# Weights of three experts loaded a stage earlier, into dead buffers, and a second buffer in the expert loop

## The reference

```python
# delta rule layer, its tail
enc = o.reshape(b, t, VAL_DIM) @ Wo
x = x + enc
h2 = _layernorm(x, ln2_g, ln2_b)
x_out = jax.nn.gelu(h2 @ W2 + b2, approximate=False) + x
...
# mixture of experts: 8 experts, each token goes to one
for ei in range(e):
    h = jax.nn.gelu(xf @ W1[ei] + b1[ei], approximate=False)   # 256 -> 1024
    y = h @ W2[ei] + b2[ei]                                    # 1024 -> 256
    mask = (idxf == ei).astype(xf.dtype)
    out = out + y * (gf * mask)[:, None]
```

## Time and profile before

| | |
|---|---|
| median of 3 runs | 699.14 us (697.95 to 700.17) |
| profiled execution | 700.65 us, of it the span 698.9 us |
| TensorE busy, share of the span | 610.0 us, 87% |
| DVE / ScalarE / Gpsimd busy | 55% / 48% / 18% |
| mean granted clock of TensorE | 0.935 |
| stage e ends, stage f starts | 578.36, 579.72 us |
| DMA moved, mean | 40.78 MB, 58 GB/s |

### The profile page before, as it was taken

One profiled execution on the slowest core, in us unless ns is written; L12 is line 12 of the kernel. 1 busy time (PEld: TensorE's weight loads), 2 busy tenths in 40 slices (PEclk: granted clock), 3 DMA queues, 4 the chain that ended last, 5 costly groups with the idle time before them and its releaser, 6 DMA issues. The chain is left out here.

```text
span 698.9 us, 20484 instructions
## 1 busy us (share of the span) xinstructions
PE 610.0 (87%) x8420; PEld 455.6 (65%) x8420; DVE 382.4 (55%) x911; ACT 333.5 (48%) x927; POOL 128.1 (18%) x192
## 2 busy tenths in 40 slices
PE   4779998999899999999777988988798986599995
PEld 2447666665466666666656765465798876498995
DVE  6426788875434545552267884879565783011211
ACT  1325655553444455444246764655365263144451
POOL 2002221001200000000223443424520204011111
PEclk9869999999999999999868999999789996799999
DMA  5950000000700000000230000000000007996110
GB/s 152 306 203 2 3 2 2 2 17 27 165 2 1 2 1 2 1 1 2 61 104 1 3 3 1 0 3 3 2 3 1 1 1 278 323 378 197 26 33 19
DMA packets 32717, 40.78 MB, mean 58 GB/s; under 512 B 8031, under 2 KB 28000, under 8 KB 32385
## 3 DMA queue, kind: packets, MB, share of 16 engines
q1 hardware_dynamic: 28672, 32.24, 14.2%
q0 software_dynamic: 1520, 4.38, 1.9%
q10 hardware_dynamic: 2448, 3.09, 1.6%
HBM read 35.33 MB, written 4.90 MB: 58 GB/s over the span
## 5 line engine op out<-in xcount | busy, mean ns | idle before, releaser
L390 ACT ACTIVATE a_pr<-a_bank,a_nms 128x160 f32<-128x160 f32 x128 | 49.2, 392 | 41.2 <-DVE a_nms L726 38.1
L2485 ACT ACTIVATE f_hb<-f_bank,cols 128x128 f32<-128x128 f32 x96 | 31.1, 368 | 59.7 <-PE f_bank L2596 38.1
L2596 PE MATMUL f_bank<-f_xts,f_w 128*128 x384 | 46.9, 282 | 9.0 <-ACT f_hb L2485 8.2
L2596 PEld LDWEIGHTS f_bank<-f_xts,f_w 128*128 128x128 f32 x384 | 46.4, 198 | 10.0 <-ACT f_hb L2485 8.4
L2606 PE MATMUL f_bank<-f_w,f_hb 128*128 128x256 f32 x192 | 46.4, 385 | 0.8 <-DVE f_yb L2565 0.8
L630 DVE TENSOR_REDUCE a_negmx<-a_bank 128x2 f32<-128x320 f32 x64 | 30.4, 475 | 22.8 <-PE a_bank L863 22.8
L2606 PEld LDWEIGHTS f_bank<-f_w,f_hb 128*128 128x128 f32 x192 | 35.3, 194 | 5.1 <-DVE f_yb L2565 1.2
L2557 DVE TENSOR_SCALAR f_xts<-f_bank 128x256 f32 x12 | 5.1, 424 | 60.8 <-PE f_bank L2588 60.8
L360 POOL TENSOR_TENSOR a_spr<-a_linv,a_hm 128x128 f32<-128x128 f32 x32 | 12.1, 400 | 123.9 <-DVE a_linv L679 111.1
L974 PE MATMUL a_bank<-b_wq,a_xtb 128*128 128x512 f32 x64 | 30.6, 624 | 2.9 <-ACT a_ct L483 2.9
L627 DVE COPY a_pt<-a_bank 128x512 f32<-128x512 f32 (+1 forms) x48 | 28.5, 593 | 7.9 <-PE a_bank L872 5.3
(11 more groups left out here) (406 smaller groups left out, 1457.8 us busy)
## 6 DMA issues: line engine op xcount, KB each, us to landing
f_w<-in_f_w SPq DMA_DIRECT2D x16, 1024.0 KB, 10.8
a_ct<-in_ctxt SPq DMA_DIRECT2D x15, 160.0 KB, 4.4
slots<-a_zero POOLq DMA_DIRECT2D x1, 2210.0 KB, 12.1
f_xs<-slots ACTq DMA_DIRECT2D x14, 130.0 KB, 2.4
rows<-in_rows SPq DMA_DIRECT2D x1, 1096.0 KB, 8.1
x<-in_x SPq DMA_DIRECT2D x2, 512.0 KB, 5.4
b_wq<-in_b_wq SPq DMA_DIRECT2D x1, 1024.0 KB, 6.2
b_wk<-in_b_wk SPq DMA_DIRECT2D x1, 1024.0 KB, 8.3
```

Of the source, the lines that this page charges most:

```text
L390: i = act.activation(pr[:, p, j, k, :], s_bank[j][:, k * KW:(k + 1) * KW], ACT.Exp, bias=nms[:, p, j, k:k + 1], accum_out=rsum[:, p, 2 * j ...
L2485: act.activation(hb[:, m, :], bank[m % 4][:, 0:P], ACT.Gelu, bias=c.col("f_b1", e * FC + m)).then_inc(z["act"], 1)
L2596: j = pe.matmul(bank[m % 4][:, 0:P], w1[:, e, kk, m * P:(m + 1) * P], xts[:, bass.ds(i % 2, 1), kk, :].rearrange("p b n -> p (b n)"), star ...
```

## The change

Three experts' weights are loaded in stage e, by a new program of SP, into buffers whose contents are no longer needed: expert 0 into `d_k` (where `aT` was) and the buffer of `lT`, once `abd` and the last factor products are done; expert 1 into `d_v`, after the last gated product; expert 2 into `e_gate`, after the last encoding. SP waits for all six transfers before the stage's end. For this `lT` becomes `c.e_lt` and stage f runs inside `held_d`. Expert 3's room is `e_wqkv` and `e_ht`, filled in stage f; experts 4 to 7 have buffers of their own.

In stage f SP waits for the scatters, loads tile 1's rows and then tile 0's, waits for tile 1's, and loads experts 3 to 7. b2 is loaded by Gpsimd into `e_xl`, and its landing counts on `stored`. `next_rows` on ScalarE moves from behind the fourth GELU to behind the eighth. DVE adds b2 into a new buffer `hy` without waiting for the store (its semaphore `yb2` is now what TensorE waits for), and waits for `rows_out` only before the product that writes `f_yb`. Gpsimd waits for the store of the tile before at the start of its tile instead of at the end of the one before.

```diff
         z = sems("eps proj ... lgs nmr ids ew")
...
+        @block.sync
+        def _(sp):
+            def weights(e):
+                sp.dma_start(c.f_w1[e], c.d["f_w1"][e, :, :].rearrange("(k p) n -> p k n", p=P)).then_inc(z["ew"], 16)
+                sp.dma_start(c.f_w2[e], c.d["f_w2"][e, :, :].rearrange("(k p) n -> p k n", p=P)).then_inc(z["ew"], 16)
+            sp.wait_ge(z["abd"], 4)
+            sp.wait_ge(z["y"], 4 * (LEVELS - 1))
+            weights(0)
+            sp.wait_ge(z["og"], NT)
+            weights(1)
+            sp.wait_ge(z["enc"], NT)
+            weights(2)
+            sp.wait_ge(z["ew"], 16 * 6)
...
         @block.sync
         def _(sp):
-            for e in range(E):
-                if e > 1:
+            sp.wait_ge(z["scattered"], 16 * NT)
+            sp.dma_start(xs[:, 1, :], slots[P:2 * P, :]).then_inc(z["xs"], 16)
+            sp.dma_start(xs[:, 0, :], slots[0:P, :]).then_inc(z["xs0"], 16)
+            sp.wait_ge(z["xs"], 16)
+            for e in range(3, E):
+                if e > 4:
                     sp.wait_ge(s_w[e - 2], 32)
-                if e == 3:
-                    sp.wait_ge(z["xs0"], 16)
-                    sp.wait_ge(z["xs"], 16)
...
         @block.gpsimd
         def _(pool):
             pool.sem_inc(z["row"], 1)
+            pool.dma_start(b2[:, :], c.d["f_b2"].partition_broadcast(P)).then_inc(z["stored"], 16)
...
             def write(e, i):
                 pool.wait_ge(z["nrm"], i + 1)
                 pool.nop(nofuse=True)
+                pool.wait_ge(z["stored"], i * 16 + 16)
+                pool.nop(nofuse=True)
+                pool.sem_inc(z["rows_out"], 1)
                 pool.tensor_copy(row[:, :], of_tile(i)[:, X_ROW:X_ROW + 1].bitcast(U32)).then_inc(z["row"], 1)
...
-                pool.wait_ge(z["stored"], i * 16 + 16)
-                pool.nop(nofuse=True)
-                pool.sem_inc(z["rows_out"], 1)
...
-            act.wait_ge(z["scattered"], 16 * NT)
-            act.dma_start(xs[:, 0, :], slots[0:P, :]).then_inc(z["xs0"], 16)
-            act.dma_start(xs[:, 1, :], slots[P:2 * P, :]).then_inc(z["xs"], 16)
...
-                    if m == 3:
-                        next_rows(i)
+                next_rows(i)
...
                 dve.wait_ge(z["ypr"], i + 1)
+                dve.wait_ge(z["yb"], i + 1)
+                dve.tensor_tensor(hy[:, :], bank[5][:, 0:D], b2[:, e * D:(e + 1) * D], ALU.add).then_inc(z["yb2"], 1)
+                dve.wait_ge(z["yb2"], i + 2)
                 dve.wait_ge(z["rows_out"], i + 1)
-                dve.tensor_tensor(yb[:, :], bank[5][:, 0:D], b2[:, e * D:(e + 1) * D], ALU.add).then_inc(z["yb2"], 1)
...
-                dve.scalar_tensor_tensor(yb[:, :], yb[:, :], kept[:, X_GATE:X_GATE + 1], kept[:, 0:D], ALU.mult, ALU.add
+                dve.scalar_tensor_tensor(yb[:, :], hy[:, :], kept[:, X_GATE:X_GATE + 1], kept[:, 0:D], ALU.mult, ALU.add
...
-                pe.wait_ge(z["yb"], i + 1)
+                pe.wait_ge(z["yb2"], i + 1)
...
             def body(e, i):
-                pe.wait_ge(s_w[e], 32)
+                if e > 2:
+                    pe.wait_ge(s_w[e], 32)
```

More of the change, by code:

```diff
@@ L2366, in stage_f @@
     with stage_semaphores(nc) as ctx:
-        sb, sem, sems, bank = stage_kit(nc, ctx, "f")
+        sb, sem, sems, _ = stage_kit(nc, ctx, "f", banks=False)
+        bank = [c.ps[:, i * 512:(i + 1) * 512] for i in range(8)]
         FC = F // P
@@ L2371, in stage_f @@
         xn = c.xn
-        w1 = sb("w1", [P, E, KC, F])
-        w2 = sb("w2", [P, E, FC, D])
+        held = len(c.f_w1)
+        w1f = sb("w1", [P, E - held, KC, F])
+        w2f = sb("w2", [P, E - held, FC, D])
+        w1 = c.f_w1 + [w1f[:, e, :, :] for e in range(E - held)]
+        w2 = c.f_w2 + [w2f[:, e, :, :] for e in range(E - held)]
+        b2 = c.f_b2
         wr, before, ones, tab, ids = c.f_small
@@ L2396, in stage_f @@
         yb = sb("yb", [P, D])
+        hy = sb("hy", [P, D])
         z = sems("lb mx sh ex se rse cand ix hot tot rank run cmp cnt zero first posa posb posh pos posi pick xn picked ends scattered "
-                 "xs0 xs nrm row rows_out xst xts hid act ypr yb2 yb stored b2")
+                 "xs0 xs nrm row rows_out xst xts hid act ypr yb2 yb stored")
         s_w = [sem(f"w{e}") for e in range(E)]
@@ L2443, in write @@
                                         bounds_check=N - 1, oob_is_err=False).then_inc(z["stored"], 16)
-                pool.wait_ge(z["stored"], i * 16 + 16)
-                pool.nop(nofuse=True)
-                pool.sem_inc(z["rows_out"], 1)
-            tiles(pool, write)
+            end = tiles(pool, write)
+            pool.wait_ge(z["stored"], end * 16 + 16)
+            pool.nop(nofuse=True)
         @block.scalar
@@ L2595, in tile @@
                     for kk in range(KC):
-                        j = pe.matmul(bank[m % 4][:, 0:P], w1[:, e, kk, m * P:(m + 1) * P],
+                        j = pe.matmul(bank[m % 4][:, 0:P], w1[e][:, kk, m * P:(m + 1) * P],
                                       xts[:, bass.ds(i % 2, 1), kk, :].rearrange("p b n -> p (b n)"),
@@ L2605, in tile @@
                     pe.wait_ge(z["act"], i * FC + (m + 5))
-                    j = pe.matmul(bank[5][:, 0:D], hb[:, m, :], w2[:, e, m, :], start=(m == 0), stop=(m == FC - 1))
+                    j = pe.matmul(bank[5][:, 0:D], hb[:, m, :], w2[e][:, m, :], start=(m == 0), stop=(m == FC - 1))
                 j.then_inc(z["ypr"], 1)
             def body(e, i):
-                pe.wait_ge(s_w[e], 32)
+                if e > 2:
+                    pe.wait_ge(s_w[e], 32)
                 tile(e, i)
@@ L2662, in build @@
             c.e_mt = sb_d("e_mt", [P, LEVELS, 32])
+            c.e_lt = sb_d("e_lt", [P, HG * NT, S])
+            flat = lambda a: a.rearrange("p a b -> p (a b)")
+            halves = lambda a: (a[:, 0:KC * F], a[:, KC * F:2 * KC * F])
+            dv, gate = c.dv[:, :, :, :].rearrange("p t e n -> p (t e n)"), flat(c.gate[:, :, :])
+            room = [(flat(c.dk[:, :, :]), flat(c.e_lt[:, :, :])), halves(dv), halves(gate),
+                    (flat(c.e_wqkv[:, :, :]), flat(c.ht[:, :, :]))]
+            c.f_w1 = [a.rearrange("p (k n) -> p k n", k=KC) for a, _ in room]
+            c.f_w2 = [b.rearrange("p (k n) -> p k n", k=F // P) for _, b in room]
+            c.f_b2 = flat(c.xl[:, :, :])
             stage_d(nc, c)
             stage_e(nc, c)
-        stage_f(nc, c, out)
+            stage_f(nc, c, out)
 def kernel(**inputs):
```

15 lines of the change are left out of this document (6 added, 9 removed).

## The result

The changed kernel took 687.66 us, the median of 4 runs (686.37, 686.40, 688.93, 690.82), against 698.92 for the kernel before beside it: a ratio of 0.9835, 95% interval 0.9805 to 0.9865. It is faster, and by more than forecast: 11.3 us instead of 7.65. So the first four executions put the gain about 2 us too high.

A forecast was written before the change was run, and what follows sets the result against it. Bound: TensorE's chain, held 8.2 us in stage f's first tile behind ScalarE's queue, with scatters slowed beside weights. First tile -8.0, stores' wait -1.35, late rows +0.5, clock +1.2: 699.14 - 7.65 = 691.5 us, range 688.8 to 695.5.

The forecast's parts named there:

- The place and the order: Stage f's first tile: GELUs follow hidden groups at once, scatters land sooner, TensorE stands 3.0 us mid-tile until the turn.
- The first tile: Start of stage f: first turn at 600.4 instead of 608.41, a gain of 8.0 us (5.0 to 9.1).
- I take 3.0: Last scatter before the first turn: lands in 3.0 us without weights beside it, instead of 6.02 (bounds 2.2 and 6.02).
- 2.4 for the rows: SP's load of tile 1's rows after the scatters: 2.4 us, the median of such loads, at least 2.1.
- The clock: TensorE's 3.0 us stand in the first tile: fall to half clock a toss-up, costing 1.2 us (0 to 2.5).
- The stores' wait: Later tiles of stage f: TensorE no longer waits for stores beside weights, gaining 1.35 us (bounds 0 and 1.35).
- Late rows: Stage f's loop: row loads issued behind the eighth GELU come late beside weights, costing 0.5 us (0 to 1.2).
- Stage e: Loading experts 0 to 2 there costs its engines nothing: 0 us (bounds 0 and 3.2).
- The rivals on fetches of instructions: Stage e: fetches delayed by weights, 3.2 us each; one gives 694.7 us (chance 0.08), five 707.5 (repeated delays: 0.04).
- The sum: All terms together, against the profiled execution: -8.0 - 1.35 + 0.5 + 1.2 = -7.65 us.
- rival (a): Stage f gains more: scatters land in 2.2 us, clock holds, rows keep pace; -10.15 us, 689.0; chance 0.12.
- the translation to the median: Whole kernel: the profiled execution's difference of -7.65 us applied to the runs' median of 699.14, giving 691.5 us.

The follow-up runs named there:

- e9: The changed kernel unaltered, third sample of its times: 689.51 us (6 runs) against 699.39 for the kernel before, ratio 0.9867.
- e0: The changed kernel unaltered, run again: 690.69 us (6 runs) against 698.59 for the kernel before, ratio 0.989.
- e3: Changed kernel with the biased sum put in the output buffer again and TensorE waiting for that: 691.88 us (7 runs), ratio 0.9902 to the kernel before.
- e7: Changed kernel with expert 0's weights loaded three times in a row in stage e; the one execution told of took 690.41 us.
- e8: Changed kernel plus ten extra first-tile matmuls, next rows behind the fourth GELU except in the first tile: 689.90 us (6 runs), ratio 0.9859 to the kernel before.
- e10: Kernel before with only the biased sum in its own buffer and TensorE waiting for that: 698.42 us (10 runs) against 699.39, ratio 0.999.
- e5: Changed kernel with the next rows normalised and loaded behind the fourth GELU again: 691.59 us (4 runs), ratio 0.9888 to the kernel before.
- e6: The kernel before, unaltered, for a second profile: 699.59 us.
- e2: Changed kernel with experts 0 to 2 loaded at the start of stage f again: 697.26 us (10 runs), ratio 0.9975 to the kernel before.
- e1: Changed kernel with the first two row loads issued by ScalarE again, after its wait for the scatters: 692.36 us (8 runs), ratio 0.9914 to the kernel before.
- e4: Changed kernel plus nine extra matmuls in TensorE's first-tile stand: 688.30 us (6 runs), ratio 0.9865 to the kernel before.

## Why the prediction was wrong, step by step

**The place and the order were right.** ScalarE's queue was freed (first GELU at 13.1), the scatter landed early, TensorE stands in the middle of the first tile for the rows, and the first turn decides the rest.

**The first tile: 8.0 forecast, 8.5 measured.** The step "I take 3.0" for the scatter and 2.4 for the rows was too high by 0.8 in sum (2.55 and 2.03); handovers took 0.3 more than my 0.15. By the Trainium skill ("DMA: Bandwidth & Descriptors", Latency and other measured facts) the estimate was a scatter shorter by 1.8 us, 4.2 us long; the trace has 2.55, less than even the stores suggested, and the measurement decides.

**The clock: +1.2 forecast as the middle of a toss-up.** The profiles show both sides: second turn 7.31 after the first where the clock held (after; 7.30 in e9), 8.96 to 8.98 where it fell (e0, e3, e7), which is 1.7 us and not 2.5, since the half clock lasted 3.4 us and not 5. In the profile after the term was zero. How often it falls over all executions is not on record: of the three profiles of the changed kernel one shows it. What I took for an independent coin has a partner that I did not see: in both profiles of the changed kernel where the clock held, ScalarE's third GELU came 1.8 us late, which broke TensorE's 2.3 us stand into two of about 1.1 and 0.6 us, and in e0, e3 and e7, without that late GELU, it fell. Nothing was made to test that link, and what delays the GELU is open. A fetch of instructions is not seen there: in after, e8 and e9 no packet of either queue of instructions (q8, q14) starts between 4 us ahead of stage f and 25 us into it.

**The stores' wait: -1.35 forecast.** Alone on the kernel before it is worth 0.8 to 1.1 (e10), undone in the changed kernel 0.65 (e3). The mechanism is right, the size is between half and all of it. The 1.35 went in full in the profile after because there the rows were in time too.

**Late rows: +0.5 forecast, 0.51 in e0, 0 in after and e9.** The load in e0 took 7.42 us to ScalarE's start, in the profile after all were in time. That the place behind the eighth GELU causes it is what e5 and e8 speak for, in one profile each.

**Stage e: 0 forecast,** 65.58 and, with three times the first load, 65.40 against 65.38 and (e6) 65.42. Right. The rivals on fetches of instructions have nothing for them, and the one that fell among the weights in e7 moved nothing. TensorE does wait 0.6 us on "issue" at 512.84 in the profile after, and in no other; its stage e is 0.2 us longer.

**The sum, and the steps that failed.** Forecast for stage f was 119.14 - 7.65 = 111.5 us. Where the clock falls it is 111.36 (e0) and 111.48 (e7); where it holds, 109.24 and 109.39. The forecast thus describes one of the two courses and was written down as their mean. That it meets e0 so closely is in part luck: there the first turn gained 8.6 us for 8.0 forecast, and the clock cost 1.7 for 1.2.

Two steps failed. The first is in the terms: the clock, put at +1.2, and the late rows, put at +0.5, both measured 0 in the profile after, and the first tile gave 8.5 for 8.0. That is 2.2 of the 3.6 us by which the first median beats the forecast (stage f gained 9.9 against 7.65), and it is the course of rival (a), which had been given 0.12. The second is the translation to the median. It had no term for what happens ahead of stage f, where the same instruction begins at 508.0 to 513.5 us, for a good part with the clock, and single executions of the changed kernel lie up to 4.5 us from their median. Compared like with like the change is worth 9.1 us; 699.14 - 9.1 = 690.0 would have been inside the range. The first four executions gave 11.3, because two of them (686.37 and 686.40) are the lowest of all 16 and only one was at the lower mean clock. So that the time fell 1.1 us out of the range is in part the draw; that the forecast was too small by 1.5 us is not. The 9.1 us lie between the 7.8 and 9.9 us that stage f gives, so nothing is left over that would need a cause ahead of it.

## What to carry to other kernels

A burst of large loads is dearest where small dependent transfers are on the path: moving 6.3 MB out of their way cut a scatter from 6.0 to 2.5 us and the load behind it from 4.3 to 2.0, and cost the stage that took them over nothing that shows. Waiting and issuing for a transfer on a compute engine's queue holds back work that doesn't need it, but freeing that queue alone only moves the stand (e2), and moving the loads alone leaves TensorE standing behind that queue (e1). Undone one at a time the two parts cost 4.9 and 6.1 us at the first turn, more in sum than the 8.5 gained, so each needs the other. When a forecast hangs on whether TensorE's clock survives a stand, give both outcomes a time and put both in the range, and add the spread of the stages that are not touched. The median of four executions was 2 us off here; comparing executions of like mean clock, or the stage in the profiles, gave the gain more closely.

## What the hardware showed that was not expected

An unbroken stand of 1.9 to 2.3 us in TensorE was followed by a fall of the clock in four executions (e0, e3, e5, e7), as were the stands of 4.8 to 8.6 us in both profiles before and in e1, e2 and e10, while two stands of 1.1 and 0.6 us were not (after, e9); the half clock then lasted 3.4 us and cost 1.7. With extra matmuls over 2.2 us of a longer stand the clock stayed at 2.4 GHz, 1.67 us of idle being left (e4). The clock also falls near 184 us in some executions of either kernel and not in others, which sets their times about 4 us apart. The indirect store lands in 5.6 to 6.0 us beside weights in the changed kernel, and in 5.8 to 6.2 before, yet the chain of stores no longer touches TensorE. And the first pass of ScalarE's loop had a hole of 1.6 to 1.8 us ahead of its third GELU in three profiles (after, e8, e9) and none in e0, e3 and e7, with the same instructions up to there.
